# Attention scores in two row groups of 64 rows, own and older block by one product, each row group writing its own PSUM bank

## The reference

```
xn  = layernorm(x)
x   = x + attention_block(xn) + expert_block(xn)

attention_block: h = layernorm(xn)*g1+b1; q (16 heads of 8), k and v (4 heads of 8), rotary q and k
    scores = q.k / sqrt(8); valid = (col <= row) & (row - col < 32); softmax; times v; Wo, bo, residual
    then layernorm, 128 -> 512 -> 128 with gelu, residual
expert_block: top 2 of 8 experts per token; silu(x w1) * (x w3), times w2, weighted sum
```

## Time and profile before

| | |
|---|---|
| time, median of 3 runs | 502.0 us (501.33 to 503.25) |
| the profiled execution | 500.98 us, of which the span of the trace is 498.8 us |
| TensorE matmul busy | 437.2 us |
| VectorE busy | 375.2 us |
| ScalarE busy | 254.9 us |
| mean granted clock of TensorE | 0.94 of full |

### The profile page before, as it was taken

How to read it: one execution, slowest core, us unless ns; L and a number is a source line. 1 busy time by engine, 2 the same in 40 slices (tenths; PEclk the granted TensorE clock), 3 DMA queues, 4 the chain that set the end, 5 groups by cost and what they waited for, 6 DMA issues and landing times. The chain is left out here.

```text
span 498.8 us, 11145 instructions
## 1 busy us (share of the span) xinstructions
PE 437.2 (88%) x3310; PEld 396.8 (80%) x3311; DVE 375.2 (75%) x1010; ACT 254.9 (51%) x536; POOL 224.5 (45%) x252
## 2 busy tenths in 40 slices
PE   2943939879999999999999999989999999997996
PEld 2832539768989898989898989989999787785873
DVE  7947555857777777777777777777877979849874
ACT  2584244454645455555546465545545737553432
POOL 3630032546464656464646465555553841312320
PEclk9985558989999999999999999999999999999799
DMA  8950123424444545343444444433450600222211
GB/s 230 260 197 0 45 87 128 148 92 145 137 145 137 149 122 156 113 144 126 147 137 138 142 142 128 143 111 132 142 143 8 166 5 1 68 60 64 64 43 42
DMA packets 38033, 57.21 MB, mean 115 GB/s; under 512 B 6238, under 2 KB 25442, under 8 KB 37872
## 3 DMA queue, kind: packets, MB, share of 16 engines
q1 hardware_dynamic: 32528, 47.66, 31.5%
q0 software_dynamic: 4608, 8.93, 5.8%
q10 hardware_dynamic: 864, 0.20, 0.2%
HBM read 48.38 MB, written 8.91 MB: 115 GB/s over the span
## 5 line engine op out<-in xcount | busy, mean ns | idle before, releaser
L1166 PE MATMUL bank<-xsT,w_sb 128*128 128x128 f32 x1008 | 132.2, 284 | 16.1 <-DVE inter L761 10.8
L1166 PEld LDWEIGHTS bank<-xsT,w_sb 128*128 128x128 f32 x1008 | 121.0, 195 | 21.9 <-issue 18.4
L409 POOL DMA_INDIRECT scratch_ys<-ysb,pair x72 | 77.1, 1071 | 124.0 <-ACT ysb L953 114.5
L402 POOL DMA_INDIRECT xsb<-scratch_xn,token x72 | 73.8, 1026 | 59.7 <-DVE token L593 35.4
L1179 PE MATMUL bank<-w_sb,inter 128*128 x576 | 79.6, 281 | 4.1 <-issue 3.3
L1179 PEld LDWEIGHTS bank<-w_sb,inter 128*128 128x128 f32 x576 | 69.9, 191 | 7.6 <-issue 7.3
L953 ACT ACTIVATE ysb<-bank 128x128 f32<-128x128 f32 x72 | 19.8, 275 | 82.7 <-PE bank L1179 79.6
L759 DVE TENSOR_TENSOR inter<-bank,act 64x128 f32<-64x128 f32 x72 | 21.2, 295 | 38.2 <-ACT act L947 32.5
L1130 PE MATMUL bank<-dv,pO 128*128 128x36 f32 x256 | 49.3, 276 | 0.6 <-ACT h2T_sb L907 0.6
L1130 PEld LDWEIGHTS bank<-dv,pO 128*128 128x128 f32 x256 | 39.6, 194 | 2.7 <-issue 2.7
L761 DVE TENSOR_TENSOR inter<-bank,act 128x384 f32<-128x384 f32 x72 | 40.2, 558 | 1.0
(11 more groups left out here) (154 smaller groups left out, 810.0 us busy)
## 6 DMA issues: line engine op xcount, KB each, us to landing
w_sb<-in_w SPq DMA_DIRECT2D x72, 448.0 KB
w_sb<-scratch_ys SPq DMA_DIRECT2D x16, 256.0 KB, 3.3
scratch_xn<-xn_sb SPq DMA_DIRECT2D x8, 256.0 KB, 4.4
w_sb<-in_w SPq DMA_DIRECT2D x1, 2048.0 KB, 9.0
out_dram<-x_sb SPq DMA_DIRECT2D x8, 256.0 KB, 2.8
xsb<-scratch_xn,token POOLq DMA_INDIRECT x72
scratch_ys<-ysb,pair POOLq DMA_INDIRECT x72
x_sb<-in_x SPq DMA_DIRECT2D x3, 256.0 KB, 3.7
```

Source lines behind the costliest of these rows:

```text
L402: nc.gpsimd.indirect_dma_start(xsb[:, j % 3, :], None, xn, bass.IndirectOffsetOnAxis(ap=token[:, j:j + 1], axis=0)).then_inc(slots_in[j % ...
L409: nc.gpsimd.indirect_dma_start(ys, bass.IndirectOffsetOnAxis(ap=pair[:, j:j + 1], axis=0), ysb[:, j % 3, :], None, bounds_check=2 * NTOK - ...
L1166: last = nc.tensor.matmul(to[:, c % EC * P:(c % EC + 1) * P], w13_sb[:, i % 3, c * P:(c + 1) * P], xsT[:, p, :], start=True, stop=True)
```

## The change

The own and the older keys of a query block lie side by side in kT, so one product with 2 x 32 keys of a group gives both. The rows are split: rows 0 to 63 hold groups 0 and 1, rows 64 to 127 groups 2 and 3. Since qbd's rows of a group meet only that group's keys, a product over 64 rows with 2 groups x 64 keys (again 128 columns) holds all that these two groups need. Row group r writes bank r. A half is now one function `scores`: 4 blocks x 2 row groups = 8 products (16 rows of trace), in the place of own_scores; nothing stands in the place of older_scores. In half 0 two small bf16 products write -1e30 over block 0's older part. Both banks are freed by `shift`, so scores(h) waits for `chosen` where own_scores waited for `own_kept`. keep_own and the copy under the mask are each cut in two, one for each bank. On VectorE, shift(k, 0) moves from behind tile 2 to behind tile 1, and values, value_steps and values_T move from behind tile 1 to behind tile 2.

```diff
@@ def shift(b, h):
-                dve.wait_ge(own_kept, 2 * b + h + 1)
-                wait_apart_dve("older_psum", older_psum, 2 * b + h + 1)
-                nc.vector.copy_predicated(half, bc(older_sb.rearrange("p (a k) -> p a k", a=1), [P, HALF * G, WIN]),
-                                          bank[1].rearrange(row, k=WIN)).then_inc(chosen, 1)
+                wait_apart_dve("own_kept", own_kept, 2 * b + h + 1)
+                parts = S[:, h].rearrange("p (n g k) -> p n g k", n=HALF, g=G)
+                for r in range(2):
+                    last = nc.vector.copy_predicated(parts[:, :, 2 * r:2 * r + 2, :],
+                                                     bc(older_sb.rearrange("p (a b k) -> p a b k", a=1, b=1), [P, HALF, 2, WIN]),
+                                                     bank[r].rearrange("p (n g c) -> p n g c", n=HALF, g=2)[:, :, :, 0:WIN])
+                last.then_inc(chosen, 1)
...
@@ VectorE, def step
                 tile(1)
                 if exists(k):
-                    values(k, p)
-                    value_steps(k, p)
-                if exists(k + 1):
-                    values_T(k + 1)
+                    shift(k, 0)
                 if exists(k - 3) and not (isinstance(k, int) and k >= B):
                     h2_of(k - 3)
                 at(1)
                 tile(2)
                 if exists(k):
-                    shift(k, 0)
+                    values(k, p)
+                    value_steps(k, p)
+                if exists(k + 1):
+                    values_T(k + 1)
...
@@ def keep_own(b, h):
-                act.wait_ge(own_psum, 2 * b + h + 1)
+                act.wait_ge(scores_psum, 2 * b + h + 1)
                 if some(b):
                     act.wait_ge(pT_ready, 2 * b)
-                nc.scalar.activation(S[:, h], bank[0], ACT.Copy).then_inc(own_kept, 1)
+                half = S[:, h].rearrange("p (n g k) -> p n g k", n=HALF, g=G)
+                for r in range(2):
+                    last = nc.scalar.activation(half[:, :, 2 * r:2 * r + 2, :],
+                                                bank[r].rearrange("p (n g c) -> p n g c", n=HALF, g=2)[:, :, :, WIN:2 * WIN], ACT.Copy)
+                last.then_inc(own_kept, 1)
...
@@ own_scores and older_scores give way to
+            def scores(b, p, h):
...
                 if h == 0:
                     pe.wait_ge(qbd_ready, b + 1)
                     pe.wait_ge(kT_ready, b + 1)
                 if some(2 * b + h):
...
                     pe.wait_ge(chosen, 2 * b + h)
                 for i in range(HALF):
                     n = HALF * h + i
...
+                    for r in range(2):
+                        rows = slice(64 * r, 64 * r + 64)
+                        last = nc.tensor.matmul(bank[r][:, i * GW:(i + 1) * GW], qbd[rows, p, n].rearrange("p h q -> p (h q)"),
+                                                kT[rows, p, 2 * r:2 * r + 2, n * WIN:(n + 2) * WIN], start=True, stop=True)
+                if h == 0:
+                    for r in range(2):
+                        last = nc.tensor.matmul(bank[r][:, 0:GW].rearrange("p (g c) -> p g c", g=2)[:, :, 0:WIN], identb_sb,
+                                                neg_sb[:, 0:GW // 2], start=True, stop=True)
+                last.then_inc(scores_psum, 1)
```

More of the change, by code:

```diff
@@ L1239, in step @@
                 if exists(k):
-                    own_scores(k, p, 0)
+                    scores(k, p, 0)
                 if exists(k + 1):
@@ L1251, in step @@
                 if exists(k):
-                    own_scores(k, p, 1)
+                    scores(k, p, 1)
                 tile_down(1)
```

27 lines of the change are left out of this document (4 added, 23 removed).

## The result

The changed kernel took 513.95 us, the median of 4 runs (512.39 to 515.22), beside 501.97 for the kernel before (501.33 to 503.25, 4 runs): a ratio of 1.0237 (95% interval 1.0209 to 1.0265). The forecast was 506.0, in a range of 500 to 520: the sign and the range held, the size did not; it was 12 us and not 4. That the range held is luck: my likeliest case reached only to 511, and 513.95 lies among the 512 to 520 us of the case in which the row groups don't overlap, which they do. The profiled execution took 513.05 us, with a span of 511.1 us against 498.8.

A forecast was written before the change was run, and what follows sets the result against it. It took waits between engines (take_xsT, gated, ScalarE's chain), not TensorE's busy time, to bound most slots. Eleven steps at a middle of +0.6 us gave +6.5, less 2 for steps 12 to 15: +4.5, 506 us, range 500 to 520.

The forecast's parts named there:

- my likeliest case: Whole kernel, row groups overlapping: +0 to +9.5 us, 502 to 511 us, middle 506; chance 0.58.
- the case in which the row groups don't overlap: Rival: each half costs 1.78 us, a step is 1.0 to 1.6 us longer, 512 to 520 us; chance 0.31.
- The saving in slot 1: Slot 1: take_xsT(2) holds the down product, so only 0.07 us of the removed products comes back.
- In slot 3 nothing comes back: Slot 3: TensorE already idles 0.65 us there, so removing the older-key products saves nothing.
- The sum of a step: A loop step with tiles was to be 0.3 to 0.9 us longer, middle 0.6.
- TensorE is the bound after all: Rival: 1.28 us a sequence comes back in slots 1 and 3, 481 us, or 497 for a quarter; chance 0.11.
- +3.5 to +9.5 us, middle 6.5: Total added over the 11 counted loop steps with tiles, at +0.3 to +0.9 us each.
- -2 us: Steps 12 to 15, without tiles: some 0.5 us saved in each, between 0 and -4 in all.
- what held it isn't told: Slot 3: take_y(1) started 0.6 us after slot 2's down product; if that stays, it is 0.7 us late.
- a sign of being wrong: Slot 2: the prediction is wrong if take_xsT doesn't end the down product's wait.
- Slot 2 was to be 0.3 us longer: Slot 2: the down product starts at about 267.2, not 266.65, behind take_xsT(3), so up_products(3) is 0.3 us late.
- A change of rows: TensorE switching between 64 and 128 rows: at least nothing, at most some 0.17 us, four times a step.

The follow-up runs named there:

- quiet sets: Sets of runs with next to no late TensorE signals; the kernel before took 490.1 to 490.9 us there, against 502.0 and 499.7 in the two others.
- queries first: take_queries put ahead of take_y(1) on ScalarE: in the changed kernel 0.9878, 0.9893 and 0.9904; in the kernel before 0.9781 with late signals, 0.9895 without.
- the second set: Set with both kernels run again unchanged, no signal late: the kernel before 490.69 us (1.0007), the changed kernel 497.8 us (1.0138).
- The test of it: Changed kernel with GpSimd's gather of tokens replaced by a plain DMA of rows 0 to 127, run twice: 499.42 us (1.0137) and 499.0 us (1.0172).

## Why the prediction missed the size

**What was right.** The row groups overlap (1.09 us for 16 rows; 1.00 was taken). The saving in slot 1 is lost to take_xsT. In slot 3 nothing comes back, since ScalarE's chain sets it. The sum of a step, +0.3 to +0.9, middle 0.6: measured 0.52 in quiet sets, 0.84 to 0.91 in the set of the result, though from other terms than mine, as said below. In the quiet sets the changed kernel was 6.9 and 10.8 us slower, with steps of the same 25.50 us in both. "TensorE is the bound after all" was wrong as a case for this kernel; with queries first it holds for slot 3 (3.29 us against 3.75), which can't be seen in the whole time.

**The step that failed** is the sum itself: "+3.5 to +9.5 us, middle 6.5", with "-2 us" for steps 12 to 15. It has no term for the clock. Three falls in the loop took 4.2 us. Step 1 took 2.4 us more with 6.8 us more at the lower level; at 1.4 us for each 3.4, an estimate, that is all of it. In the last stretch I got 1.0 us back of the 2, and there too the clock has a share. The mechanism of the other 6.8 us stood in the text. Which idle time brings a fall about wasn't to be read from the trace of before, where TensorE's clock fell once in steps 1 to 11; but a cost of 1.4 us a fall could have been worked out from the pace at half the clock, and the range, not the middle, would have carried it.

**Mis-sized terms.** Slot 3: "what held it isn't told. If nothing does now ... only keep_own's +0.16 goes on ... If the 0.6 us stays, it is 0.55 + 0.16 = 0.7 us late". It was 0.96 in the set of the result, since the late signal doubled to 1.19 us, and 0.40 in quiet ones, of which keep_own is 0.07. I had put the down product's delay down to take_xsT(3) behind h2, and had named it as a sign of being wrong if another wait ended last there. It did, narrowly: the 16 rows and the changes of rows let the down product start 0.05 us later than take_xsT(3) would have. Slot 2 was to be 0.3 us longer and was 0.06. For take_xsT(3) I had added 264.0 + 2.33 + 0.57 + 0.28 = 267.18 without taking off the overlaps that I name, 0.2 us or so, and its second masked copy costs 0.04 and not 0.16. A change of rows costs 0.20 us, where I had allowed for 0 to 0.17: the first scores row starts 0.20 behind the transpose, the second pair 0.21 behind the first, the down product 0.21 behind the last pair and its second row 0.21 behind its first, where 0.11 is the pace. That second row starts at 268.75; without scores it could start two rows behind the transpose, at 267.24 + 0.22. A half so costs 1.29 us of TensorE and not 1.00. Here the rule of the Trainium skill, "TensorEngine Tiling (Array Packing)", section Key Properties, that changing the mode drains TensorE, agrees with the trace, and the same page's parallel tiles do too. The gap behind the first row isn't peculiar to 64 rows: where a down product has waited, as in slot 1 of the kernel before (259.40 in the second set), its second row starts 0.21 us behind the first too. Slot 4 came out 0.2 us shorter in steps without a fall, not 0.16 longer: in step 7 of before GpSimd's short instruction started inside VectorE's subtraction ahead of take_xsT(5), which took 0.99 us (from 273.71); now it starts ahead of it, and the subtraction takes 0.72.

**Open.** What holds TensorE's signals in two of six sets. They fall into GpSimd's indirect DMAs or just behind them in all cases, which is a coincidence in time and no proof; records of signals are missing in the same traces, so that the recording itself may have a part in it. The test of it met only quiet sets. Open too is what brings a fall of the clock about.

## What to carry to other kernels

Ask of a wait not only which engine ended it but what stands on that engine ahead of the awaited instruction and doesn't need to: four instructions moved on ScalarE gave more than the row groups did, in either kernel (0.978 to 0.990 of the time before with the move, in the changed kernel and in the one before). A saving on the busiest engine comes back only in slots where its own list ends last, and the list of before can show this: slot 3 of the kernel before had 0.2 us to give in a quiet set. And idle time that a change opens on TensorE can come with a lower clock afterwards; where the gain is 1%, read the granted clock by stretches before reading anything else.

## What the runs showed of the hardware

- Products of two groups of 64 rows, taking turns, start in pairs 0.01 us apart, a pair each 0.11 us; four of one group and then four of the other need 1.64 us for the 16 rows and not 1.10. A product of 128 rows and 256 columns needs 0.22 us a row.
- A change between 128 and 64 rows costs two gaps of 0.10 us, one at the first row of the new kind and one behind it. The second is there also behind the first row after a wait.
- In some sets a quarter to a third of TensorE's signals were recorded 0.1 to 2.2 us late or not at all; in the others none was late, and at most four of some 240 in a trace were missing. This goes for the same kernel: a step of the kernel before takes 25.79 us in the one and 24.98 in the other.
- VectorE's 128x512 subtraction (0.69 us) took 1.31 us when an instruction of GpSimd started 0.54 us into it, 0.99 when it was 0.22 us, and 0.72 when GpSimd had started just before it. A gather or scatter alone beside it cost it nothing (264 cases, 0.69 to 0.75 us). GpSimd's addition behind it took 1.19 to 1.20 us and not 0.74.
